# Rows of four projection blocks by transposing DMAs of 16-bit halves, joined on ScalarE

## The reference, cut to what matters

```python
x = x + attn(cond(x, cond_512, ...), ...)     # first step: its result is called x1 below
x = x + ffn(cond2(x, ids, ...), rhs)          # second step works on x1
# the end of attn, where the change sits:
g2 = gelu(h2 @ mlp_gate_w.T + mlp_gate_b);  f2 = h2 @ mlp_fc_w.T + mlp_fc_b
return f2 * g2 @ out_w.T + out_b + hs2        # p = f2*g2 has 1536 channels, the result 512
```

## Time and profile before

| what | value |
|---|---|
| median of 3 runs | 1754.11 us (1750.48 to 1755.96) |
| the profiled execution, its device time | 1751.69 us |
| its span, first to last instruction | 1749.7 us |
| TensorE busy | 1735.5 us, 99% |
| VectorE, ScalarE, GpSimd busy | 1186.4, 879.7, 790.3 us |
| TensorE clock granted | 0.997 of full speed |
| DMA traffic | 233.37 MB, mean 133 GB/s |

### The profile page before, as it was taken

How to read it: one execution, slowest core, us unless ns; L and a number is a source line. 1 busy time by engine, 2 the same in 40 slices (tenths; PEclk the granted TensorE clock), 3 DMA queues, 4 the chain that set the end, 5 groups by cost and what they waited for, 6 DMA issues and landing times. The chain is left out here.

```text
span 1749.7 us, 23284 instructions
## 1 busy us (share of the span) xinstructions
PE 1735.5 (99%) x7927; PEld 1414.9 (81%) x7935; DVE 1186.4 (68%) x1753; ACT 879.7 (50%) x1301; POOL 790.3 (45%) x702
## 2 busy tenths in 40 slices
PE   9999999999999999999999999999999999999998
PEld 7888888888788888888888888778887887887886
DVE  7766666669979678686563335357886687677555
ACT  7655556565666575674562222243553443443433
POOL 1122221222677566665550000015577877878742
PEclk9999999999999999999999999999999999999999
DMA  6011100120233424322546668877645445544511
GB/s 207 1 49 49 48 26 22 49 73 25 97 120 118 147 97 162 103 96 79 187 144 215 196 195 281 325 260 237 217 133 188 135 158 173 154 158 148 167 38 61
DMA packets 121030, 233.37 MB, mean 133 GB/s; under 512 B 25138, under 2 KB 25394, under 8 KB 120932
## 3 DMA queue, kind: packets, MB, share of 16 engines
q1 hardware_dynamic: 90772, 156.65, 26.7%
q0 software_dynamic: 11776, 41.95, 7.1%
q10 hardware_dynamic: 18384, 33.56, 5.8%
HBM read 169.73 MB, written 58.72 MB: 131 GB/s over the span
## 5 line engine op out<-in xcount | busy, mean ns | idle before, releaser
L1068 PE MATMUL bank<-h_parts,mlp_w 128*128 128x512 f32 x2016 | 461.1, 390 | 3.3 <-DVE gelu L1561 2.5
L1068 PEld LDWEIGHTS bank<-h_parts,mlp_w 128*128 128x128 f32 x2016 | 379.2, 188 | 83.9 <-DVE gelu L1561 2.9
L353 PE MATMUL bank<-h_parts,gate_w 128*128 128x512 f32 x1536 | 351.1, 389 | 0.6 <-DVE h_parts L688 0.6
L353 PEld LDWEIGHTS bank<-h_parts,gate_w 128*128 128x128 f32 x1536 | 288.1, 188 | 61.9 <-issue 0.9
L2066 PE MATMUL bank<-operand_parts,int_w 128*128 128x512 f32 x1152 | 281.8, 394 | 1.3 <-DVE x_columns L1594 1.1
L1133 PE MATMUL bank<-p_parts,mlp_out_w 128*128 128x512 f32 x1152 | 271.2, 393 | 0.0
L1133 PEld LDWEIGHTS bank<-p_parts,mlp_out_w 128*128 128x128 f32 x1152 | 213.7, 188 | 48.4 <-issue 4.2
L2066 PEld LDWEIGHTS bank<-operand_parts,int_w 128*128 128x128 f32 x1152 | 213.1, 188 | 45.3 <-issue 2.1
L615 POOL TENSOR_TENSOR decay_sq<-decay 128x512 f32<-128x512 f32 x32 | 39.3, 1228 | 278.8 <-DVE decay L701 278.8
L1406 POOL TENSOR_TENSOR product_out<-product_out,gelu 128x512 f32<-128x512 f32 x69 | 121.0, 1774 | 93.1 <-DVE product_out L1561 92.5
L1286 ACT ACTIVATE product_copy<-bank,vec_sb 128x512 f32<-128x512 f32 x144 | 99.1, 688 | 105.2 <-PE bank L1068 103.9
(11 more groups left out here) (311 smaller groups left out, 2768.8 us busy)
## 6 DMA issues: line engine op xcount, KB each, us to landing
p_tile<-p_d ACTq DMA_DIRECT2D x96, 256.0 KB, 4.8
p_d<-product_out SPq DMA_DIRECT2D x92, 256.0 KB, 2.0
raw_mlp_w<-mlp_gate_g SPq DMA_DIRECT2D x21, 512.0 KB, 3.6
raw_mlp_w<-mlp_fc_g SPq DMA_DIRECT2D x21, 512.0 KB, 4.4
xin<-xT SPq DMA_DIRECT2D x8, 1024.0 KB, 6.8
hs_d<-u SPq DMA_DIRECT2D x8, 1024.0 KB, 5.0
hs_pair<-hs_d SPq DMA_DIRECT2D x8, 1024.0 KB, 7.5
x_columns<-xT SPq DMA_DIRECT2D x8, 1024.0 KB, 6.8
```

The lines of the kernel that those rows point to most:

```text
L353: i = pe.matmul(bank[:], gw[:, w, s, k, m * P:(m + 1) * P], hr[:, q, t, k, :], start=k == 0 and n == 0, stop=k == KT - 1 and n == 2)
L1068: i = pe.matmul(bank[:], wb[g % 2][:, s, w, kk, :], hop[u % 2][o][:, t, kk, :], start=first and kk == 0 and n == 0, stop=kk == 1 and n == ...
```

## The change

For blocks 0 to 3 (`TURNED = NB - 4`), TensorE's transposes and ScalarE's four copies out of PSUM are gone. In their place, during the next block:

- `turn`: SyncE issues four transposing DMAs (one for each 128 channels). Each reads 128 channels x 512 fp32 seen as 1024 numbers of 16 bits, and writes 1024 rows of 128 such numbers, so that even rows hold the low and odd rows the high halves of the tokens.
- `split_halves`: after all four have landed, four plain DMAs on chip bring the halves to partitions by token: 64 partitions each, runs of 1 KB.
- `join_halves`: ScalarE, at its j = 8, 9, 10 and 11 (`JOIN_ACT`), writes low and high halves into the interleaved 16-bit places of the row buffer: two copies of 128x512 for each token tile.
- On SyncE, the four transposing DMAs go ahead of the store of xt, the four plain ones behind it; the load of the next x waits for the store and the transposing DMAs, no more for TensorE. Row buffers move to 48 KB, and weight slot 4 is loaded after slot 5 and after the last of these rows is stored.

```diff
+TURN_AT, JOIN_AT, TURNED = 72 * KB, 48 * KB, NB - 4
...
+    turned = at("x1_turned", [P, 2 * TT, D], TURN_AT, U16)
+    halves = at("x1_halves", [P, TT, 2, D], HF_AT, U16)
...
+    JOIN_ACT = {8: 0, 9: 1, 10: 2, 11: 3}
...
+        def turn(b):
+            sp.wait_ge(halves_there, 64 * b)
+            for k in range(KT):
+                sp.dma_start(turned[:, :, k * P:(k + 1) * P], xt[:, k, :].bitcast(U16), transpose=True).then_inc(turn_done, 16)
+
+        def split_halves(b):
+            sp.wait_ge(turn_done, 64 * (b + 1))
+            sp.wait_ge(t_evac, TT * b)
+            for odd in range(2):
+                for h in range(2):
+                    sp.dma_start(halves[64 * odd:64 * odd + 64, :, h, :], turned[h:P:2, odd:2 * TT:2, :]).then_inc(halves_there, 16)
...
                 sp.wait_ge(r1, KT * b)
+                if b - 1 < TURNED:
+                    turn(b - 1)
                 sp.dma_start(x1T_d[:, :, bass.ts(b - 1, BT)], xt[:]).then_inc(x_stored, 16)
+                if b - 1 < TURNED:
+                    split_halves(b - 1)
                 sp.wait_ge(x_stored, 16 * b)
-                sp.wait_ge(t_ps, TT * b)
+                if b - 1 >= TURNED:
+                    sp.wait_ge(t_ps, TT * (b - TURNED))
             sp.dma_start(xt[:], xT[:, :, bass.ts(b, BT)]).then_inc(x_loaded, 16)
...
-                if b and j in TOK_PE:
+                if b - 1 >= TURNED and j in TOK_PE:
                     to_tokens(b - 1, TOK_PE[j])
...
+        def join_halves(b, t):
+            act.wait_ge(halves_there, 64 * (b + 1))
+            act.wait_ge(t_stored, 16 * b)
+            row = rows_of[b][:, t, :].bitcast(U16).rearrange("p (d h) -> p d h", h=2)
+            act.activation(row[:, :, 0], halves[:, t, 0, :], ACT.Copy)
+            act.activation(row[:, :, 1], halves[:, t, 1, :], ACT.Copy).then_inc(t_evac, 1)
...
         def early_slots():
-            for j in (2, 3, 4, 5):
+            for j in (2, 3, 5):
                 load_slot(j)
+            sp.wait_ge(mlp["tok_stored"], 16 * TURNED)
+            load_slot(4)
```

More of the change, by code:

```diff
@@ L8 @@
 I32 = mybir.dt.int32
+U16 = mybir.dt.uint16
 ALU = mybir.AluOpType
@@ L889, in mlp_half @@
     xt = at("x_columns", [P, KT, BT], XT_AT)
-    rows_of = [at("x1_rows", [P, TT, D], HF_AT)] * (NB - 2) + [at("x1_rows_late", [P, TT, D], G2)]
+    rows_of = ([at("x1_rows_joined", [P, TT, D], JOIN_AT)] * TURNED + [at("x1_rows", [P, TT, D], HF_AT)] * (NB - 2 - TURNED)
+               + [at("x1_rows_late", [P, TT, D], G2)])
+    turned = at("x1_turned", [P, 2 * TT, D], TURN_AT, U16)
+    halves = at("x1_halves", [P, TT, 2, D], HF_AT, U16)
     o_loaded = [sem(f"mlp_out_w_loaded{n}") for n in range(3)]
@@ L894, in mlp_half @@
     p_high, p_low, o_ps = sem("p_high"), sem("p_low"), sem("mlp_out_ps")
+    turn_done, halves_there = sem("x1_turn_done"), sem("x1_halves_there")
     t_ps, t_evac, t_stored = sem("x1_tok_ps"), sem("x1_tok_evac"), sem("x1_tok_stored")
@@ L1001, in visit, with store_rows @@
                 store(i, t)
+        def turn(b):
[8 more added lines that the diff above has]
+                    sp.dma_start(halves[64 * odd:64 * odd + 64, :, h, :], turned[h:P:2, odd:2 * TT:2, :]).then_inc(halves_there, 16)
+        def store_rows(b):
+            sp.wait_ge(t_evac, TT * (b + 1))
+            sp.dma_start(x1_d[:, bass.ds(TT * b, TT), :], rows_of[b][:]).then_inc(t_stored, 16)
         def load_hs2(b):
@@ L1032, in body @@
             if b:
-                sp.wait_ge(t_evac, TT * b)
-                sp.dma_start(x1_d[:, bass.ds(TT * (b - 1), TT), :], rows_of[b - 1][:]).then_inc(t_stored, 16)
+                store_rows(b - 1)
             if b == LAST_FIRST + 1:
@@ L1125, in project_out @@
                         pe.wait_ge(r1, KT * (b - 2) + c + 1)
-                        pe.wait_ge(t_evac, TT * (b - 1))
+                        if b - 2 >= TURNED:
+                            pe.wait_ge(t_evac, TT * (b - 1))
                     if b == NB - 2 and c == 2:
@@ L1330, in group @@
                 gelu_of(g, 1)
+        def join_halves(b, t):
[4 more added lines that the diff above has]
+            act.activation(row[:, :, 1], halves[:, t, 1, :], ACT.Copy).then_inc(t_evac, 1)
         def evacuate_rows(b, t):
-            act.wait_ge(t_ps, TT * b + t + 1)
-            act.wait_ge(t_stored, 16 * b)
+            act.wait_ge(t_ps, TT * (b - TURNED) + t + 1)
+            if b > TURNED:
+                act.wait_ge(t_stored, 16 * b)
             if b == NB - 2:
@@ L1343, in body @@
                     tile_high(n)
-                if b and j in TOK_ACT:
+                if b and b - 1 < TURNED and j in JOIN_ACT:
+                    join_halves(b - 1, JOIN_ACT[j])
+                if b - 1 >= TURNED and j in TOK_ACT:
                     evacuate_rows(b - 1, TOK_ACT[j])
@@ L2274, in last_rows_out @@
             for t in ts:
-                act.wait_ge(mlp["tokens"], LAST_ROWS + t + 1)
+                act.wait_ge(mlp["tokens"], TT * (NB - 1 - TURNED) + t + 1)
                 act.activation(last_rows[:, t, :], ring[2 + t % 2][:], ACT.Copy).then_inc(mlp["tok_evac"], 1)
```

## The result

The changed kernel takes 1777.68 us (median of 4 runs, 1771.16 to 1780.54) against 1752.83 us before: 24.9 us slower, ratio 1.013, 95% interval [1.0113, 1.0147]. The forecast was 1748.1 with a range to 1765. The profiled execution has a span of 1775.7 us, 26.0 more than before.

A forecast was written before the change was run, and what follows sets the result against it. TensorE's instruction stream was taken to bound the kernel. Transposes gone -7.5, no stall in blocks 1 to 3, 1.5 us stall in block 4: -6.0 us, 1754.1 to 1748.1 us; range 1744.5 to 1765.

The forecast's parts named there:

- What goes: TensorE's transposes in four blocks: 0.47 us a token tile, 1.88 us a block, 7.5 us off its stream, blocks of 32.65 us.
- The due times: After SyncE passes r1 at t, halves are due for ScalarE's joins at t + 20.6, next x for VectorE at t + 24.0.
- Issue of the transposing DMAs, 2.4 us each, landed by t + 11.7: On SyncE: issue between 1.20 and 2.4 us each, 2.4 taken; four issued by t + 9.7, last landed at t + 11.7.
- "Between 19 and 88 ns by size lies 49 ns: 3.1 us": The plain DMAs' 1024 packets of 1 KB: 49 ns each, 3.1 us; 5.6 us if each costs as much as 2 KB.
- "both run into the next block by some 2 us, which the slow issue of the transposing DMAs hides": Later row stores and hs2 behind them overrun each block by some 2 us, hidden by the transposing DMAs' issue.
- "the trace never shows two of them back to back, and one took 7.4 us": Argument for transposing DMAs not overlapping: no back-to-back pair in the trace, and one took 7.4 us among other traffic.
- Block 4, 1.5 us of stall: SyncE passes r1 2.1 us late behind small loads, 1 MB just ahead: halves 0.9 late, x 1.1 late; 1.5 us stall.
- A stall costs its own length: In the sum, stalls were added to TensorE's time at their own length: -7.5 + 3 x 0 + 1.5 = -6.0 us.
- Rival B: Transposing DMAs on SyncE run in single file, four take 19.2 us, landing later than about t + 13: +20, 1774; 0.20 with worse.
- Rival A: Plain DMAs' 1 KB packets cost 88 ns, halves 1.2 late, x 1.4 late: +0.7, 1754.8 us; 0.31 with what lies between.
- Rival C: Each 128x128 piece costs an issue, 32 of 1.20 us on SyncE, halves at t + 48: +102, 1856 us; chance 0.02.
- Margins: In blocks 1 to 3 halves 1.3 us and x 1.1 us ahead of due, so no stall; stalls under 2.3 us: 0.47.

The follow-up runs named there:

- run 3: The changed kernel with its four plain DMAs over all 128 partitions on both sides instead of 64, same bytes: 1749.67 us, 0.998 of before.
- 8: The changed kernel with plain DMAs writing to every second partition, and the change for blocks 0 to 2 only: 1748.36 us, 0.9961 of before; repeated 1749.33 us.
- 10: The changed kernel with plain DMAs writing to every second partition, and hs2 loaded behind the load of x in blocks 1 to 3: 1753.11 us, 0.9997.
- 11: The changed kernel for blocks 0 to 2 only, every second partition as target, hs2 loaded behind the load of x: 1749.63 us, 0.9981 of before.
- run 13: Kernel 10 with the FFN's first x1 tiles (1 MB) loaded in block 3, not ahead of block 4's transposing DMAs: 1746.72 us, 0.9962 of before.
- run 4: The changed kernel with joins at ScalarE's tile 11 and the next block's tiles 0 to 2, rows stored after that block's x load: 1788.87 us, 1.0208.
- run 9: The changed kernel with the next hs2 loaded behind the load of x in blocks 1 to 3: 1768.31 us, 1.0089 of before.
- kernels 5: The changed kernel with plain DMAs writing to every second partition instead of 64 neighbours, rows stored in two DMAs a block: 1754.16 us, 0.9998 of before.
- run 1: The kernel before, plus the 16 transposing DMAs issued beside TensorE's transposes, their result not used: 1754.27 us, 1.0004 of before.
- run 6: The changed kernel with plain DMAs also reading 64 neighbouring partitions instead of every second one: 1758.68 us in one run.

## Why the prediction was wrong, by its own steps

- *What goes*: right. With the halves in time three blocks are 32.64 us each, as predicted (runs 3, 8, 10, 11, 13), and run 13 gets 6.6 of the 7.5 us.
- *The due times* t + 20.6 and t + 24.0: right. In block 1 the join started 1.3 us late and TensorE waited 1.3; in run 4 x was 1.8 late and TensorE waited 1.9.
- *Issue of the transposing DMAs, 2.4 us each, landed by t + 11.7*: too dear for a free queue. Four took 6.2 us and landed by t + 8.7; the price is nearly one per instruction, the lower end named.
- *"Between 19 and 88 ns by size lies 49 ns: 3.1 us"*: this is the step that failed first. By size it was right (46 to 48 ns with the target spread). The plain DMAs of the change write to 64 neighbouring partitions, and there a packet took 110 ns in block 1 and up to 155 in block 4 (1097 to 1105 us), above the upper bound of 88. I had bounded the packet by its size alone and not by where it goes.
- *"both run into the next block by some 2 us, which the slow issue of the transposing DMAs hides"*: this failed and cost more. The late rows and hs2 aren't hidden by the issue; they make it longer, 11.0, 8.5 and 15.8 us. Late halves make late joins and a late hs2 load, these a slow issue, and that later halves. Run 9 shows this part for blocks 2 and 3 (9.7 us), runs 10 and 13 for block 4 (7.7 us of wait, then 0.5).
- *"the trace never shows two of them back to back, and one took 7.4 us"*: misread. The trace of before has seven pairs 1.2 to 1.3 us apart, and five of them are issued 0.5 us behind a 1 MB load of x1 tiles on the same queue. Its SyncE at 1438 us, and the tile's view of 1438.6 to 1441 us, with issue (ns) and landing:

```profile
1438.29 0.38 SPq L1855 DMA_DIRECT2D x_tiles<-x_d  x1
1438.81 8.86 SPq L1873 DMA_TRANSPOSE q_transposed<-q_tile  x3
```

```profile
L1873 SPq DMA_TRANSPOSE q_transposed<-q_tile x2: 1195/1263/1331, 1438.8 to 1440.1; - x2
...
DMA to landing us min/median/max: 6.2/6.5/6.9
```

  The ten of these five pairs land in 6.2 to 7.4 us; the pair at 1693.7 us, with no load ahead, in 2.4 and 2.5. So what a load just ahead does to a transposing DMA stood in the trace, as its landing; a longer issue doesn't show there, with two at a time.
- *Block 4, 1.5 us of stall*: the order of events was right, the 1 MB issued just ahead was seen, its price wasn't: 12.9 us of wait.
- *A stall costs its own length*: it cost a third more. Behind the waits the granted clock went to its lower level, 1.2 GHz, for parts of blocks 2 to 4, and some 8 us of the 24.6 are lost there. Short waits went either way: behind 2.28 us in block 4 of run 3 and 1.75 in block 1 of run 9 the clock stayed at 1.00, behind 1.95 us in block 1 of run 4 and 1.82 in block 3 of run 9 it fell (0.95 over the block).
- *Rival B*, 1774, is near in time, and its sign came: in blocks 2 to 4 the four landed at t + 15.9, t + 13.6 and t + 19.9, later than t + 13. But its reason, that they don't overlap, is wrong: in block 1 they landed at t + 8.7, and run 9 has them fast in three blocks. *Rival A* named the dear packet; it priced it at 88 ns without what follows from it. That its halves, 1.2 us late, are so near to block 1's 1.3 is luck: a faster issue and dearer packets cancel. *Rival C* didn't come: 8 pieces of 128x128 went in one issue of 1.26 us at the shortest.
- *Margins*: two chains with 1.1 and 1.3 us to spare over three unknown prices were read as "no stall" with 0.47. They should have been read as a coin's throw, with a loss that grows from block to block on one side.

Open: what makes the issue of the transposing DMAs long behind a load, as the runs show only that it goes with the load's place; and why single runs of kernels 5 and 10 spread over 11 to 13 us. That block 4's wait comes in some and not in others would fit the profiles and the 4 us of run 13, but only one execution of each was seen.

## What to carry to other kernels

Price a DMA by where it goes as well as by its packets: before a plain on-chip DMA is put ahead of a due time, look whether its target is spread over the partitions (46 against 110 ns a packet here). When work moves off the bounding engine into a queue, give the chain its due times as here, and then ask what one missed due time does to the next round; if it delays transfers that stand in front of the same chain, move those first. A block-wise profile (length, wait, clock, issue time in each block) tells such a loop from a constant cost: here only the first block showed the bare price.

## What the runs showed of the hardware

- A transposing DMA of 128 x 1024 in 16 bits, on chip, took 1.24 us of issue at the shortest (run 1; 1.26 in the change), against 1.19 to 1.20 for 128 x 512: twice the bytes, nearly the same issue.
- 1 KB packets on chip, in the windows of the plain DMAs: 45 to 56 ns to all or to every second partition, 69 to 90 ns to 64 neighbours from 64 neighbours (run 6), about 80 to 155 ns to 64 neighbours from every second.
- Four transposing DMAs whose start fell within 5.5 us of the issue of a 1 MB load took 9.1 to 15.8 us of issue (12 cases of the runs 1 to 10 and the change), 7.8 us or more behind it 5.6 to 6.7, but 8.4 in run 13's block 4.
- ScalarE's 16-bit copies with a stride of two on the output took 0.75 to 0.78 us each, but followed each other at 0.65 (979.90, 980.55).
